# Fourth expert mixture: the running sum moves from VectorE to GpSimd

## The reference, cut to what matters

```
h1 = gelu(einsum('td,edh->teh', flat, rw1) + rb1)          # 8 routed experts, hidden width 256
expert_out = einsum('teh,ehd->ted', h1, rw2) + rb2
mixed = einsum('ted,te->td', expert_out, weights)          # weights: 0 but for the top 2
x = x + (gelu(flat @ sw1 + sb1) @ sw2 + sb2) + mixed       # the shared expert has no weight
```

## Time and profile before

| what | us |
|---|---|
| median of 3 executions (2007.34 to 2012.43) | 2007.45 |
| profiled execution, its own time | 2016.02 |
| span of the profiled execution | 2014.3 |
| TensorE busy in the span | 1817.5 (90%) |
| VectorE busy in the span | 1520.5 (75%) |
| GpSimd busy in the span | 786.9 (39%) |

### The profile page before, as it was taken

How to read it: one execution, slowest core, us unless ns; L and a number is a source line. 1 busy time by engine, 2 the same in 40 slices (tenths; PEclk the granted TensorE clock), 3 DMA queues, 4 the chain that set the end, 5 groups by cost and what they waited for, 6 DMA issues and landing times. The chain is left out here.

```text
span 2014.3 us, 29655 instructions
## 1 busy us (share of the span) xinstructions
PE 1817.5 (90%) x10579; PEld 1223.9 (61%) x10579; DVE 1520.5 (75%) x2730; ACT 1007.3 (50%) x1492; POOL 786.9 (39%) x640
## 2 busy tenths in 40 slices
PE   4988999679999999999998999879789999979798
PEld 2556888444444444444445777645457789957676
DVE  6677996767677767676757888799799965567698
ACT  2555888445666566656644555435400120045586
POOL 2332331156777676766662344233202402012131
PEclk8997999779999999999997999889989999989799
DMA  1001211100000000000000212000000010000032
GB/s 64 1 0 26 105 64 53 50 0 1 1 1 1 1 1 1 1 1 1 1 1 19 85 63 84 12 1 0 17 11 26 32 53 0 0 12 0 6 127 95
DMA packets 21179, 51.27 MB, mean 25 GB/s; under 512 B 3563, under 2 KB 11383, under 8 KB 18116
## 3 DMA queue, kind: packets, MB, share of 16 engines
q1 hardware_dynamic: 20596, 49.53, 7.2%
q10 hardware_dynamic: 464, 0.20, 0.0%
HBM read 48.48 MB, written 1.25 MB: 25 GB/s over the span
## 5 line engine op out<-in xcount | busy, mean ns | idle before, releaser
L1513 POOL TENSOR_TENSOR sb_L_total<-sb_L_total,sb_L_probT 128x512 f32<-128x512 f32 (+1 forms) x192 | 267.1, 1415 | 50.5 <-ACT sb_L_probT L1817 46.6
L395 POOL TENSOR_TENSOR sb_L_prob<-sb_L_prob,sb_L_rsum 128x616 f32<-128x616 f32 (+1 forms) x96 | 98.1, 1043 | 270.0 <-DVE sb_L_rsum L637 270.0
L1817 ACT ACTIVATE sb_L_probT<-banks 128x1024 f32<-128x1024 f32 x128 | 131.1, 1025 | 139.0 <-PE banks L1646 138.6
L1874 DVE TENSOR_REDUCE sb_L_top_tok<-banks 128x2 f32<-128x1024 f32 x128 | 155.9, 1220 | 25.7 <-PE banks L1613 25.7
L1656 PE MATMUL banks<-sb_L_probT,sb_L_v 128*64 128x512 f32 x512 | 138.2, 619 | 0.2 <-DVE sb_L_mixedT L1925 0.2
L1510 POOL TENSOR_TENSOR sb_L_total<-sb_L_probT 128x512 f32<-128x512 f32 x64 | 80.7, 1281 | 131.0 <-ACT sb_L_probT L1817 131.0
L543 ACT ACTIVATE sb_L_probT<-banks 77x512 f32<-77x512 f32 x160 | 89.7, 589 | 76.9 <-PE banks L446 76.9
L2238 DVE SCALAR_TENSOR_TENSOR sb_L2f_hid<-banks,sb_L2f_weight,sb_L2f_hid 128x512 f32<-128x512 f32 x176 | 122.5, 744 | 2.5 <-PE banks L97 1.6
L2308 DVE SCALAR_TENSOR_TENSOR sb_resid<-banks,sb_L2f_weight,sb_resid 128x128 f32<-128x128 f32 x192 | 67.1, 351 | 62.5 <-PE banks L97 57.9
L1218 DVE TENSOR_TENSOR sb_L0f_hid_low<-sb_L0f_raw,sb_L0f_hid_high 128x1024 fp32r<-128x1024 f32 x64 | 88.7, 1401 | 29.4 <-ACT sb_L0f_hid_high L1176 29.0
L432 PE MATMUL banks<-sb_L_kdiag,sb_L_qT 128*128 (+2 forms) x192 | 84.9, 584 | 21.2 <-DVE sb_L_prob L628 10.1
(11 more groups left out here) (411 smaller groups left out, 5227.3 us busy)
## 6 DMA issues: line engine op xcount, KB each, us to landing
sb_L0f_wide<-spread_L0f SPq DMA_DIRECT2D x7, 1024.0 KB, 5.8
sb_L1f_wide<-spread_L1f SPq DMA_DIRECT2D x7, 1024.0 KB, 7.5
sb_L3f_wide<-spread_L3f SPq DMA_DIRECT2D x7, 1024.0 KB, 5.4
sb_fetched<-L2f_w SPq DMA_DIRECT2D x12, 256.0 KB, 2.6
sb_fetched<-L1f_gu SPq DMA_DIRECT2D x8, 336.0 KB, 3.0
sb_fetched<-L0f_w SPq DMA_DIRECT2D x8, 259.0 KB, 2.7
sb_fetched<-L0f_w SPq DMA_DIRECT2D x8, 256.0 KB, 3.5
sb_normT<-L2f_w SPq DMA_DIRECT2D x2, 768.0 KB, 5.5
```

Of the source, the lines that this page charges most:

```text
L395: pool.tensor_tensor(grid, grid, bcast(rsum[:, i % PROBS, half], [None, KEYS]), ALU.mult).then_inc(normed, 1)
L1513: pool.tensor_tensor(sums[rows], sums[rows], probT[rows, k, h], ALU.add).then_inc(added[h], 1)
L1817: act.activation(probT[:, k], ps[:, slot:slot + 2, :], ACT.Exp).then_inc(exped, 1)
L1874: dve.tensor_reduce(top_tok[:, :, k:k + 1].rearrange("p h k -> p (h k)"), ps[:, banks:banks + 2, :], AX.X, ALU.max).then_inc(bound_read, 1)
```

## The change

Two conditions are changed in `dense_experts` and one is simplified. Before, only the gated kind (`L1f`) handed its additions to GpSimd; now every kind that is not folded does, which adds `L3f` to them. `L0f` (folded) keeps its additions on VectorE, and for it the last edit changes nothing, since its `FIRST` is 0.

```
@@ gpsimd: the loop over the steps
                 for s in range(1, STEPS):
-                    if s >= BATCH and gated:
+                    if s >= BATCH and not folded:
                         add(s)
                     if s % BATCH == BATCH - 1 and s + BATCH + 1 < STEPS:
                         part_first(s // BATCH + 2)
...
@@ vector: combine(s)
-                        if gated and s >= BATCH + HALVES:
+                        if not folded and s >= BATCH + HALVES:
                             dve.wait_ge(combined, s - BATCH - 1)
...
-                        if gated:
+                        if not folded:
                             return
-                        if e == 1 and FIRST == 0:
+                        if e == 1:
                             dve.wait_ge(weighed, b + 1)
```

## The result

The changed kernel takes 2028.07 us (median of 4 executions, 2023.98 to 2033.72) against 2008.32 us for the kernel before (4 executions, 2007.34 to 2012.43). The ratio is 1.0096, with a 95% interval of 1.0067 to 1.0126: about 19 us slower (13.5 to 25.3). The forecast was 15.7 us slower, about 2023.

What follows compares the result with a forecast made beforehand. TensorE was taken to bound the fourth mixture's steady part. First-half splits 12.6, second-half splits 2.1 and the end 1.3, less 0.3 gained, made 15.7 us on 2007.45: about 2023, range 2010.5 to 2030.5.

Steps and rivals of the forecast that it cites:

- TensorE is the bound and can win only 0.3: Fourth mixture's steady part: TensorE is busy throughout, so relieving VectorE can win at most 0.3 us.
- The place in the queue, six waits for L1021: First-half weight splits queued behind additions on GpSimd: TensorE waits for experts 3 to 8, 6 x 2.1 = 12.6 us.
- 8.39: Microseconds after the start of step 4k + 3 on TensorE when expert k + 2's hidden matmuls start, needing its first-half weights.
- The floor of 0.41: Least stall per expert for first-half weights, in us, from queue order alone with GpSimd undisturbed; six times makes 2.5.
- `part_second`, 7 x 0.3: Second-half weight splits behind additions on GpSimd: TensorE waits seven times, experts 2 to 8, 2.1 us in all.
- The gain of 0.3: Removing 32 additions from VectorE gains 0.3 us in the fourth mixture's steady part.
- The end, 1.3: End of the fourth mixture: longer GpSimd additions, with `hid_low` of step 35 waiting, start the last sum 1.3 us later.
- The rule on the shared port: VectorE with two SBUF inputs and GpSimd reading SBUF block each other; full-duration hand-overs would add 1.4 us, not booked.
- A: Rival: the engines disturb each other little, only queue order costs; +2.8 to +6 us, about 2011.5; chance 0.13.
- B: Rival: additions, `hid_low` and splits saturate the VectorE and GpSimd pair; +20 to +28 us, about 2031; chance 0.11.
- C: Rival: not slower, GpSimd works ahead so weights aren't late; 2007.5 to 2008 us; chance 0.04.
- D: Rival: the change frees something large, of about 6 us; chance 0.02.

Runs made afterwards that it cites:

- e3: Changed kernel with weight splits moved ahead of additions in GpSimd's queue and `hid_low`'s second input from PSUM (a timing probe): ratio to before 1.0000, length 99.32 us.
- e10: Kernel before, all additions on VectorE, with only `hid_low`'s second input from PSUM from step 6 on (a timing probe): ratio to before 0.9999, length 98.39 us.
- e2: Changed kernel, queue order kept, with `hid_low`'s second input from PSUM from step 6 on (a timing probe): ratio to before 1.0016, length 102.92 us.
- e7: Changed kernel with only the first weights' splits (`part_first`) moved ahead of an addition in GpSimd's queue: ratio to before 1.0040, length 109.74 us.
- e4: Kernel before with only the last four additions (steps 32 to 35) given to GpSimd: ratio to before 1.0008, length 99.98 us.
- e8: Changed kernel with only the second weights' splits (`part_second`) moved ahead of an addition in GpSimd's queue: ratio to before 1.0072, length 116.67 us.
- e1: Changed kernel with both weight splits moved one or two additions forward in GpSimd's queue, additions still on GpSimd: ratio to before 1.0022, length 102.81 us.
- e6: Changed kernel with both weight splits moved forward in GpSimd's queue and the last four additions back on VectorE: ratio to before 1.0026, length 101.77 us.
- e5: Changed kernel with the last four additions back on VectorE, additions 4 to 31 still on GpSimd: ratio to before 1.0077, length 113.06 us.
- e9: Kernel before with additions 33 and 34 on GpSimd, outputs of steps 34 and 35 before all transposes, shares before last sums: ratio to before 1.0002, length 98.34 us.

## Why the prediction was right

- *TensorE is the bound and can win only 0.3.* Right as a bound: e3 and e10 win 0.35, with VectorE 24 or 3 us lighter. But the prediction booked the 0.3 to the additions that leave VectorE, and e10 wins it without moving any.
- *The place in the queue, six waits for L1021.* Right in number, line and size. The path of one expert as predicted, against the trace for expert 7: share late by 0.7, measured 0.63 (TensorE's step would have put its end at 1979.54 - 8.39 + 6.11 = 1977.26; it ended at 1977.89); addition 0.07 behind it, 0.08; `hid_low` 1.07 behind the addition, 1.08; `w1_high` 0.53 behind that, 0.47; `w1_low` 0.72, 0.72; the stall 2.1, 2.05. The mean over six is (9.7 + 6 x 0.17) / 6 = 1.79, so the term was 10.7 and not 12.6: I had carried the late share of one case to all six. It holds for the last four (2.04 to 2.14); the first two were 0.66 and 1.74.
- *The floor of 0.41.* 0.50 in e2, where the port is free.
- *`part_second`, 7 x 0.3.* Its sum is right (1.8 for 2.1), its form isn't: two waits, not seven, and the size depends on the other halves (e7).
- *The gain of 0.3* did not come in the changed kernel: its small gaps outside the waits are 0.3 us, as before. 12.5 of the 13.4 us are waits with a named releaser, and 0.8 the slower start behind each, which the prediction did not have.
- *The end, 1.3.* The step is right for the additions (e4: 1.26), but as the term of the changed kernel it was mis-sized: 3.49. Missing in it were the late VectorE, since I started from before's times at the end of the steady part (with the additions 1.89, e8), and the stretch at the lower clock level (1.60). With VectorE late, the order that I had predicted is turned round: `hid_low` of step 35 came first (2007.82, 1.23 us), and the two additions took 3.48 together.
- *ScalarE's wait for `hid_low`* (8.4 us, 5 times) was not foreseen. It follows TensorE's stalls. Whether it prolongs them wasn't tried.
- *The rule on the shared port* (the Trainium skill, SBUF — State Buffer, "Who interferes with whom": the loser blocks for the whole of the other's instruction). The trace agrees on the block. It has `hid_low` end 1.08 behind the addition, not its full 1.23, and the path with 1.07 holds to 0.05; so the hand-over does not cost the loser's full duration. That the two wait for each other, and that an input from PSUM ends it, e2 shows.
- *Rivals.* A (only the order costs, +2.8 to +6): its price is right for e2, where the port is free (+3.24 in the steady part, +4.20 in all), and the changed kernel is not that case. B (saturation): not what the changed kernel loses to, since GpSimd there waits 25.7 us for shares, and the same work in e1's order is 11.5 us shorter; what e1 still loses is of its kind, TensorE waiting for a stretched L1218. C (not slower): refuted, the share ended late and the weights were late at 8.39. D: nothing of that size exists, e3 ends at 0.35.

The sum of the mixture was 15.7 for 16.85 measured, 14.4 for 13.36 in the steady part and 1.3 for 3.49 at the end: two errors that partly cancel. The mechanism was right, and that the sum came within 1.2 us is in part luck. The forecast for the time also started from a median of three executions, 2007.45; later groups of the same kernel had medians of 2009.51 to 2011.17.

## What to carry to other kernels

Before work goes to an engine that is idle on average, put its queue in order of time: find what the bounding engine wants from behind the new instruction, when the new instruction's input is ready, and whether that is early enough. Then look at what the new instruction runs beside, since VectorE instructions with two SBUF inputs and GpSimd's instructions stand for each other; a late place in the queue and a shared port cost 3.6 and 2.2 us alone and 13.7 together. The order is free to choose, so the splits belong ahead of the additions; but even then nothing is won if the engine that was relieved did not bound the stage.

## What the runs showed that was not expected

- One PSUM input removes the contention: with it, 30 `hid_low` lay between 1220 and 1222 ns beside additions with a median of 1293, while with two SBUF inputs they reached 2224.
- The two engines can lock into a round without idle time: two additions and two splits in 5.87 us in e1, repeated, for 2 x 1.29 + 0.61 + 0.64 = 3.8 us of undisturbed work.
- In the changed kernel and in e1, e6 and e7, TensorE's clock was at the lower level for 3.4 us in the end of the mixture; in before, e2, e3, e4, e5, e9 and e10 it was not. The ends with it had a wait of TensorE before the transposes of 2.1 to 3.8 us, those without 1.2 to 1.9 but for e5 and e8 (2.3 and 3.8, clock 1.00), so the wait alone doesn't decide it. In e8 three stretches of 3.4 us had it in the steady part, the first from 1932.2, behind a stall of 1.92 us for L1021 that ended at 1930.75; the changed kernel had four stalls of 2.04 to 2.14 in its steady part and kept 1.00. This stays open.
